# Four maximum pieces in every step, and an earlier load of q and k, in a causal attention kernel

## What is computed

```python
xn = layernorm(x)
q, k, v = split(xn @ w_in.T)            # 16 heads of 16
att = where(causal, q @ k.T / 4, 0.0)   # the masked scores are 0, not -inf
att = softmax(att)
out = x + (att @ v) @ w_out.T + ffn(xn)
```

## Time and profile before

| what | us |
|---|---|
| median of 3 runs (1253.02 to 1254.95) | 1254.49 |
| the profiled execution | 1255.49 |
| its span, first to last instruction | 1253.7 |
| PE busy | 1138.2 |
| DVE busy | 963.7 |
| ACT busy | 743.4 |
| POOL busy | 360.0 |

### The profile page before, as it was taken

How to read it: one execution, slowest core, us unless ns; L and a number is a source line. 1 busy time by engine, 2 the same in 40 slices (tenths; PEclk the granted TensorE clock), 3 DMA queues, 4 the chain that set the end, 5 groups by cost and what they waited for, 6 DMA issues and landing times.

```text
span 1253.7 us, 26837 instructions
## 1 busy us (share of the span) xinstructions
PE 1138.2 (91%) x7168; PEld 473.4 (38%) x7168; DVE 963.7 (77%) x2433; ACT 743.4 (59%) x1553; POOL 360.0 (29%) x716
## 2 busy tenths in 40 slices
PE   2999888879999999999989999998999999999998
PEld 1656554433333333333333333333333333333345
DVE  5776788869689958986878589868886887689722
ACT  1454333256766666666556666675567667666773
POOL 6122111332323232324122323241224133314221
PEclk9999899979999999999989899999899999899999
DMA  2576633308100900190009001900090028002033
GB/s 92 137 206 170 190 118 104 108 11 114 36 2 13 137 6 2 23 128 7 3 10 140 7 2 20 130 7 3 16 135 7 2 35 116 6 2 77 5 103 108
DMA packets 62010, 79.57 MB, mean 63 GB/s; under 512 B 6688, under 2 KB 52128, under 8 KB 60832
## 3 DMA queue, kind: packets, MB, share of 16 engines
q1 hardware_dynamic: 60704, 73.56, 29.3%
q0 software_dynamic: 1152, 4.19, 1.1%
HBM read 43.78 MB, written 29.36 MB: 58 GB/s over the span
## 4 chain that ended last, share of the span: by engine, by line
PE 53%; issue 13%; DVE 9%; POOL 2%; ACT 1%; DVEq 1%; POOLq 0%; DMA 0%; SPq 0%; ACTq 0%
PE ps_o L1090 17%; PE ps_s L1076 15%; PE ps_m L228 14%; DVE part_max L243 4%; PE ps_m L1122 2%; PE ps_o L1100 2%; DVE ps_m L239 2%; POOL after L220 1%; DVE row_max L256 1%; DVE part_max L239 1%; ACT probs L958 1%; PE ps_x L1067 1%; PE ps_x L1068 1%; DVE turned L993 1%; PE ps_x L1053 1%
## 5 line engine op out<-in xcount | busy, mean ns | idle before, releaser
L958 ACT ACTIVATE probs<-ps_s 128x512 f32<-128x512 f32 (+3 forms) x1280 | 610.3, 535 | 307.2 <-PE ps_s L1076 302.3
L243 DVE TENSOR_REDUCE part_max<-ps_m 128x1 f32<-128x512 f32 x730 | 474.2, 681 | 37.5 <-PE ps_m L228 36.0
L1076 PE MATMUL ps_s<-q_op,k_op 99*128 99x512 bf16 (+3 forms) x1280 | 435.0, 358 | 15.8 <-issue 7.3
L228 PE MATMUL ps_m<-k_op,q_op 96*128 96x512 bf16 (+3 forms) x1200 | 405.1, 357 | 34.3 <-DVE part_max L243 24.3
L239 DVE CUSTOM_DVE_ANT_0 ps_m<-ps_m,mask 128x384 f32<-128x384 f32 x470 | 229.8, 497 | 135.0 <-PE ps_m L228 132.7
L1090 PE MATMUL ps_o<-probs,v_sb 128*32 128x512 f32 (+3 forms) x2560 | 306.5, 552 | 6.9 <-POOL probs L906 6.9
L906 POOL TENSOR_SCALAR_AFFINE_SELECT probs<-probs 128x128 f32<-128x128 f32 x512 | 142.4, 293 | 412.4 <-ACT probs L958 405.6
L1076 PEld LDWEIGHTS ps_s<-q_op,k_op 99*128 99x128 bf16 x1280 | 122.6, 98 | 337.4 <-ACT probs L958 221.9
L228 PEld LDWEIGHTS ps_m<-k_op,q_op 96*128 96x128 bf16 x1200 | 118.5, 99 | 191.8 <-DVE part_max L243 86.3
L873 POOL TENSOR_TENSOR diag_weight<-ident,masked_weight 128x2048 f32<-128x2048 f32 x32 | 115.4, 3607 | 122.7 <-ACT masked_weight L925 122.7
L1090 PEld LDWEIGHTS ps_o<-probs,v_sb 128*32 128x32 f32 x2560 | 51.2, 109 | 96.4 <-issue 39.7
(11 more groups left out here) (84 smaller groups left out, 871.1 us busy)
## 6 DMA issues: line engine op xcount, KB each, us to landing
parts_d<-parts SPq DMA_DIRECT2D x48, 256.0 KB, 3.1
q_op<-parts_d SPq DMA_DIRECT2D x42, 256.0 KB, 13.6
k_op<-parts_d SPq DMA_DIRECT2D x42, 256.0 KB, 15.1
vpad_d<-v_pad SPq DMA_DIRECT2D x32, 256.0 KB, 3.5
v_sb<-vpad_d SPq DMA_DIRECT2D x8, 1024.0 KB, 26.2
x_in<-x SPq DMA_DIRECT2D x8, 512.0 KB, 5.4
ffn_d<-ffn SPq DMA_DIRECT2D x8, 512.0 KB, 3.2
attn_t<-normed SPq DMA_DIRECT2D x128, 32.0 KB, 2.3
```

What stands on the lines that cost most here:

```text
L228: last = pe.matmul(ps_m[:, f % ring, 0:width], self.q_op[0:ROWS, p, h, q0:q0 + P], self.k_op[0:ROWS, p, h, pc * CH:pc * CH + width], start ...
L243: dve.tensor_reduce(self.part_max[:, u % 2, h * SUB + s, pc:pc + 1], ps_m[:, f % ring, 0:width], AX_X, ALU.max).then_inc(self.piece_reduce ...
L958: act.activation(probs[:, slot % PRING, 0:width], ps_s[:, slot % SRING, 0:width], ACT.Exp).then_inc(probs_ready, 1)
L1076: pe.matmul(ps_s[:, slot % SRING, 0:CH - q0], k_op[0:KROWS, p, h, kt * P:(kt + 1) * P], q_op[0:KROWS, p, h, u * CH + q0:(u + 1) * CH], sta ...
```

## The change

The pieces come one per head step throughout: head step n of a group has piece (84 + n) mod 160, of this group for n below 76 and of the next from 76 on (unit 2, step 19). PE's wait for the next group's q and k moves from the begin of unit 3 to the first of the next group's pieces. SP issues the 12 loads of q and k at the begin of a group, behind a wait for all score tiles of the group before, and the load of the values where all 13 were. Two of the `SHIFT_AT` entries move. Through `HEAD_START`, 84 pieces instead of 80 are done beside the tokens.

```diff
-HEAD_START = PIECE0[2] + 32
-SLOT_PIECES = {0: (HEAD_START, PIECE0[3]), 1: (PIECE0[3], PIECE0[3] + 32),
-               2: (PIECE0[3] + 32, PIECES), 3: (0, HEAD_START)}
-SLOT_SPREAD = {0: 16, 1: 32, 2: 30, 3: 64}
+AHEAD_FROM = 19
+HEAD_START = PIECES - 4 * AHEAD_FROM
-SHIFT_AT = {(3, 5): 0, (3, 11): 1, (1, 2): 2, (2, 8): 3}
+SHIFT_AT = {(3, 3): 0, (3, 10): 1, (1, 2): 2, (2, 8): 3}
-def pieces_of(slot, head_step):
-    lo, hi = SLOT_PIECES[slot]
-    n, spread = hi - lo, SLOT_SPREAD[slot]
-    at = min(head_step, spread)
-    return range(lo + n * at // spread, lo + n * min(at + 1, spread) // spread)
+def piece_at(u, kt, h):
+    ahead, f = divmod(HEAD_START + GH * (KT0[u] + kt) + h, PIECES)
+    return f, ahead
 # SP, a group
             def group(i, p, first=False, last=False):
+                if not last:
+                    if not first:
+                        sp.wait_ge(scores_ready, (i * 2 + p) * SLOTS)
+                    ops.load_scores(sp, i + p, 1 - p)
                 if not first:
                     keep_normed(i - 1 + p, 1 - p, NCH - 1)
                 place_shift(p, 2, unit_of(i, p, 2))
                 if not last:
                     sp.wait_ge(out_ready, unit_of(i, p, 0) + 1)
-                    ops.load_group(sp, i + p, 1 - p)
+                    ops.load_values(sp, i + p, 1 - p)
 # DVE, a head step
-                        if not (nxt and last):
-                            for f in pieces_of(u, hs):
-                                ops.reduce_piece(dve, ps_m, MRING, f, base)
-                                ops.after_piece(dve, f, unit_of(i, p, nxt), base, f + 1 == PIECES)
+                        f, ahead = piece_at(u, hs // GH, hs % GH)
+                        if not (ahead and last):
+                            base = (G + ahead) * PIECES
+                            ops.reduce_piece(dve, ps_m, MRING, f, base)
+                            ops.after_piece(dve, f, unit_of(i, p, NCH * ahead), base, f + 1 == PIECES)
 # PE, a head step
-                            if not (nxt and last):
-                                for f in pieces_of(u, kt * GH + h):
-                                    ops.score_piece(pe, ps_m, MRING, f, 1 - p if nxt else p, (G + (nxt > 0)) * PIECES)
+                            f, ahead = piece_at(u, kt, h)
+                            if not (ahead and last):
+                                if ahead and f == 0:
+                                    pe.wait_ge(q_loaded[1 - p], ops.loaded(1 - p, i + 1 + p))
+                                    pe.wait_ge(k_loaded[1 - p], ops.loaded(1 - p, i + 1 + p))
+                                ops.score_piece(pe, ps_m, MRING, f, 1 - p if ahead else p, (G + ahead) * PIECES)
```

More of the change, by code:

```diff
@@ L185, in set_constants, with load_scores @@
                       allow_small_or_imprecise_dtypes=True).then_inc(self.consts_made, 1)
-    def load_group(self, sp, i, p):
+    def load_scores(self, sp, i, p):
         for r in range(len(Q_PARTS)):
@@ L192, in load_group @@
             sp.dma_start(self.k_op[rows, p], self.parts_in[K_PARTS[r], 1, i, p]).then_inc(self.k_loaded[p], 16)
-        self.load_values(sp, i, p)
     def load_chunk(self, sp, i, p, c):
@@ L1016, in group @@
                 for u in range(NCH):
-                    nxt = NCH if u == NCH - 1 else 0
-                    base = (G + (nxt > 0)) * PIECES
                     for hs in range(key_tiles(u) * GH):
-                        if not (nxt and last):
-                            for f in pieces_of(u, hs):
-                                ops.reduce_piece(dve, ps_m, MRING, f, base)
-                                ops.after_piece(dve, f, unit_of(i, p, nxt), base, f + 1 == PIECES)
+                        f, ahead = piece_at(u, hs // GH, hs % GH)
[3 more added lines that the diff above has]
+                            ops.after_piece(dve, f, unit_of(i, p, NCH * ahead), base, f + 1 == PIECES)
                         if NORM_AT <= hs < NORM_AT + NORM_STEPS and not (first and u == 0):
@@ L1132, in group @@
                     pe.wait_ge(shift_loaded[u % 2], (G * (NCH // 2) + u // 2 + 2) * SHIFTS)
-                    if nxt and not last:
-                        pe.wait_ge(q_loaded[1 - p], ops.loaded(1 - p, i + 1 + p))
-                        pe.wait_ge(k_loaded[1 - p], ops.loaded(1 - p, i + 1 + p))
                     for kt in range(key_tiles(u)):
```

## The result

| | before | after |
|---|---|---|
| median of 6 runs each, us | 1253.76 (1243.82 to 1258.31) | 1293.42 (1287.32 to 1294.81) |
| the profiled execution, us | 1255.49 | 1290.18 |
| its span, us | 1253.7 | 1288.4 |
| mean granted clock | 0.970 | 0.955 |

What follows compares the result with a forecast made beforehand. PE, busy 91% with 53% of the chain, was taken as the bound, so only its waits and lower clock could change. Eight terms summed to +14 on the profiled 1255.49 us, giving 1269.5 us, range 1234 to 1284.

Steps and rivals of the forecast that it cites:

- terms 4 and 5: Five pieces become four in unit 3 and unit 2's first steps, -22; end of unit 2 gets pieces, +1.
- terms 2 and 6: Lower PE clock behind the holds: unit 0 +4.5, end of unit 2 +7, besides the latter's hold, +18.
- Terms 7 and 8: Loads at the two jumps back, +2; four more pieces beside the tokens and four fewer in the last group, +1.
- Term 1: Unit 0: POOL's long instruction holds a small DVE instruction longer, +2.2 us in each of 8 groups, +17.6.
- Term 6: End of unit 2: a new hold of a small DVE instruction by POOL, +18, and +7 of lower clock.
- Term 3: Values land in time, so PE's waits for POOL's blocks at the end of unit 2 and their lower clock go, -15.
- term 5: End of unit 2 gets pieces: fills PE's waits, but six small DVE instructions behind piece 159 delay the next; +1.
- Rival (c): Loads starve the instruction fetch at the jumps or all along, +8 or more there, 1277 us; chance 0.09.
- (a): Hold only in unit 0, none at the end of unit 2: 1244.5 us; chance 0.20.
- (b): No hold at all, DVE goes first everywhere and the present unit 0 waits go too: 1204 us; chance 0.08.
- (d): Evens out: clock falls no more often, DVE catches up before the holds, gains and losses meet: 1255 us; chance 0.08.

Runs made afterwards that it cites:

- The loads alone: Kernel before with q and k loaded at the group's begin, values behind unit 2's shift, pieces where they were; 1259.68 us, 1.005 of before.
- The pieces alone: Kernel after with all 13 loads back at their old place; 1291.94 us, 1.031 of before.
- Unit 2's shift two steps earlier: Against a variant of after (AHEAD_FROM 18, values at the group's begin, q and k behind unit 2's shift): that shift at step 4, not 6; 1218.07 us.
- the last run: Against "Unit 2's shift two steps earlier": five of the six small instructions behind piece 159 go one each behind the following pieces; 1217.75 us.
- one step later: Kernel after with AHEAD_FROM 20 instead of 19, pieces four head steps later; 1269.04 us, 1.015 of before.
- one step earlier: Kernel after with AHEAD_FROM 18 instead of 19, pieces four head steps further ahead; 1237.85 us, 0.987 of before.
- `diag_weight` in quarters: Kernel after with POOL's one 2048-column diag_weight instruction cut into four of 512, positions unchanged; 1241.5 us, 0.991 of before.

## Why the prediction was wrong

It had the sign and the mechanism of the loss, and missed the size by 20.7 us: 9.4 in the holds, 11.3 in the gain. The steps that failed are terms 4 and 5 (-21 together forecast, -3.4 measured) and the clock of terms 2 and 6 (11.5 forecast, about 24 measured). Terms 7 and 8 came out lower than forecast, which hid a part of it.

1. *Term 1, the hold in unit 0.* Right: before's L260 (now L253) is caught, 0.26 us behind POOL's start where I had 0.5, and PE waits 2.9 to 3.3 us. With term 2 it was to be +22.1; measured +26.4.
2. *Terms 2 and 6, the clock: mis-sized.* I gave every hold 1.5 us of lower clock and the border a chance of 0.7. No hold was spared. Over 13 us at 0.83, and over 11 us at 0.69, work of 2.2 and 3.4 us is lost at most. In sum, PE's long waits in the two places went from 11.4 us to 43.7 (8 of 1.85 to 3.30, 7 of 2.75), which is 32 of the 56.4; about 24 are left for the slower clock and what follows on it, where I had 11.5. The mean clock allows for that: (1 - 0.955) x 1288.4 less (1 - 0.970) x 1253.7 is 20.4 us over the whole kernel, although the end of unit 2, 0.89 or 0.77 over 15 us in four groups before, is now at full clock. The Trainium skill ("SBUF — State Buffer", Who interferes with whom) names both instructions that were caught, `tensor_scalar` and `cast`, among those that can need the shared port pair, and `tensor_reduce` not. That is what the rows show: L253 3.40, L260 3.60, while L236 and L245 never grew.
3. *Term 6, the border.* The mechanism is right, before's L267 (now L260) is caught in seven of seven, the middle one of the three I named; PE waits 2.75 where I took 2.6. With the clock +30.0 instead of +25.
4. *Term 3, the values: right alone, void together.* "The loads alone" shows -13.5 at the end of unit 2 against my -15. "The pieces alone" shows that with pieces there late values cost nothing. So the -15 can't be added to term 5: with pieces there, the stretch is as long with late values.
5. *Terms 4 and 5, five pieces become four: the step that failed.* I took -22 for unit 3 and the begin of unit 2 and gave the end of unit 2 only +1. Measured against "the loads alone", which has the values in time as well: unit 3 -28.2, the end of unit 2 +22.0, steps 6 to 19 +2.8, together -3.4. Of the 28.2, some 14 are the own time of 13 pieces a group that left (an estimate: 0.22 us for 512 columns, narrower ones in proportion). At the end of unit 2 there are 17 more a group, by the same estimate some 19 of the 22.0. So what is really gained in unit 3 is some 14, not 18; at the end of unit 2 some 3 come on top of the moved work, where I had +1; and the begin of unit 2 brings no 4 us, since steps 6 to 19 grow although they have a piece less. "Unit 2's shift two steps earlier", where no hold and no late load disturbs, says the same: -27.1, +20.9 and +1.7 against "the loads alone", together -4.5. Timelines of DVE and PE at the end of unit 2:

```profile
578.00 0.70 DVE L232 CUSTOM_DVE_ANT_0 ps_m<-ps_m,mask 128x512 f32<-128x512 f32 x1 [0.83 <-PE ps_m L221]
```

```profile
578.81 0.34 PE L221 MATMUL ps_m<-k_op,q_op 96*128 96x384 bf16 x1 [0.36 <-DVE part_max L232]
...
581.59 0.39 PE L221 MATMUL ps_m<-k_op,q_op 96*128 96x512 bf16 x1 [0.52 <-DVE part_max L232]
```

   In each step DVE stands for 0.8 us while PE does `weigh_values`, and then PE stands for 0.4 to 0.5 us because DVE is behind. I read this as three buffers that don't bridge the 1.07 us of `weigh_values`; no run had more of them. Term 5 also named the wrong cause at piece 159. The step there takes 3.53 us where the next take 2.88, 0.7 a group and near my 1.0, but it is the wait of piece 0 for all pieces before it, which the prediction didn't have, and not the six small instructions: the last run shows that spreading them gives nothing.
6. *Terms 7 and 8.* At the jumps +2 forecast; the stretch that has them got 2.1 us shorter in all, and the two jumps against their neighbours about 1 us longer. Term 8 was +1; the -3.1 and -0.6 in its place are no effect of the change that a run shows, and luck for the sum. Rival (c), which I gave 0.09, is real in its neighbours: 22 us in "the loads alone" and in "one step later".
7. *Rivals (a), (b), (d)* fell: in each place one of DVE's instructions met POOL's in every group, and the clock fell behind it. What (b) described is the kernel with step 18, and there it is worth 55.6 us.

**Left open.** Why the loads at the jump cost DVE 10.8 to 11.0 us of waiting for issue in two kernels, 4.9 at one jump of after and none in "one step earlier" and in "`diag_weight` in quarters", although q and k start there each time. Without loads at the jump (before, "the pieces alone") it isn't there; 1 MB instead of 3 was tried only with pieces that didn't have it with 3 either. That "issue" is the supply of instructions is my reading. And why "unit 2's shift two steps earlier" has no wait for issue between the jumps, though its 3 MB are under way in steps 6 and 7 too, wasn't looked into.

## What to carry to other kernels

Before moving small VectorE instructions, list the long GpSimd instructions and the order of both within a step: a scaling of 0.2 us that starts 0.3 us behind a GpSimd instruction of 3.6 us lasts 3.4 us, and a shift by one step of the loop was worth 55.6 us here. Cutting the long instruction in four (+0.4 us of its own) gave back 51.9 us without moving anything. When a pass is spread evenly, count the moved work where it arrives as well as where it leaves, ask whether the buffers bridge the longest stretch in which the producer does something else, and look for waits that were free only because a pause lay in front of them.

## What the runs showed of the hardware

- Waits for issue and transfers: with 3 MB of loads in flight, engines stood with nothing to wait for that the profile shows, PE 1.3 to 3.4 us five times in straight code of "one step earlier", DVE 10.8 us behind a jump back in "the loads alone". With 1 MB at that place PE's five were gone, and one of 1.60 us came at step 17, where the 3 MB were then in flight. Loads in flight aren't enough for it: "unit 2's shift two steps earlier" had none between the jumps.
- The granted clock fell behind every one of PE's 2.75 us waits, to 0.84, 0.70 or 0.69 over 11 us, and in before already behind five of eight waits of 1.4 us. Of 56.4 us, some 32 were in the waits and some 24 behind them.
- A GpSimd instruction cut into four pieces of 128x512 took 4.03 us against 3.61, and DVE's instructions got in between the four, held 0.83 and 0.88 us in unit 0 and 1.05 at most.
- `tensor_scalar` and `cast` on 128x16 elements took 0.20 us alone and up to 3.42 and 3.65 us beside a GpSimd `tensor_tensor` of 3.61 us; the small `tensor_reduce` took 0.22 us at most everywhere.
